# First mean layer of a four-layer graph network: products made in the normalising stage, gathered by the edge sums

## The reference, cut to what matters

```python
x1 = layernorm(x + L0(x, ...))            # (50000, 128)

def sage_conv(h, src, dst, n, W_self, W_neigh, b):
    agg  = segment_sum(h[src], dst, n)
    deg  = segment_sum(ones, dst, n)
    mean = agg / maximum(deg, 1.0)[:, None]
    return h @ W_self + mean @ W_neigh + b

h1 = relu(sage_conv(x1, src, dst, n, W_self1, W_neigh1, b1))   # the part that changes
x2 = layernorm(x1 + sage_conv(h1, src, dst, n, W_self2, W_neigh2, b2))
```

## Time and profile before

| | us |
|---|---|
| median of 3 runs (8755.55 to 8763.08) | 8756.22 |
| the profiled execution | 8752.19 |
| its span | 8750.5 |

### The profile page before, as it was taken

The page is one execution under the profiler, slowest core; times in us unless marked ns, Lnnn a source line. Parts: engine busy times, 40 slices in busy tenths (PEclk is TensorE's granted clock), DMA queues, the critical chain, the costliest instruction groups (busy, mean ns, idle before and its releaser), DMA issues. The chain is left out here.

```text
span 8750.5 us, 136064 instructions
## 1 busy us (share of the span) xinstructions
PE 5075.0 (58%) x26949; PEld 3942.2 (45%) x26950; DVE 4064.5 (46%) x13584; ACT 2826.8 (32%) x6967; POOL 4235.5 (48%) x4934
## 2 busy tenths in 40 slices
PE   3666667705679556965785567544444444414577
PEld 2555444504568445854564455333322233303555
DVE  3555558861222122755662227544444444452458
ACT  0544452361343124841331248311111111100239
POOL 4777750056630565036615664555555555507650
PEclk7766679955789567976896679666666666655679
DMA  1222225572358223943574458311111111122348
GB/s 31 65 66 66 67 60 173 183 242 64 93 156 248 70 85 116 337 161 101 156 230 120 118 169 288 117 49 53 47 48 49 48 48 48 48 20 61 90 149 295
DMA packets 610422, 1013.48 MB, mean 116 GB/s; under 512 B 174962, under 2 KB 177296, under 8 KB 610064
## 3 DMA queue, kind: packets, MB, share of 16 engines
q1 hardware_dynamic: 279472, 417.77, 16.1%
q10 hardware_dynamic: 197568, 359.75, 11.6%
q0 software_dynamic: 133280, 234.88, 10.9%
HBM read 648.88 MB, written 363.07 MB: 116 GB/s over the span
## 5 line engine op out<-in xcount | busy, mean ns | idle before, releaser
L447 PE MATMUL agg_bank<-agg_msgs,agg_onehot 128*128 x7840 | 1573.5, 361 | 976.0 <-issue 697.9
L447 PEld LDWEIGHTS agg_bank<-agg_msgs,agg_onehot 128*128 128x128 f32 x7840 | 1344.7, 256 | 1273.3 <-issue 1263.5
L385 DVE TENSOR_TENSOR agg_onehot<-iota,rel 128x512 f32<-128x512 f32 x1176 | 814.3, 692 | 1717.5 <-issue 630.3
L316 POOL DMA_INDIRECT agg_msgs<-y,agg_rows x784 | 784.3, 1000 | 409.3 <-issue 210.9
L1446 PE MATMUL score_look<-score_rounded,score_loT 128*128 128x392 bf16 x392 | 178.5, 455 | 716.9 <-ACT score_loT L1515 535.1
L1398 POOL DMA_INDIRECT by_source<-score_line,score_places x392 | 397.3, 1013 | 261.7 <-DVE score_line L1572 152.7
L482 ACT ACTIVATE agg_kept<-agg_bank,inv_root 128x128 f32<-128x128 f32 x784 | 226.5, 367 | 879.9 <-PE agg_bank L447 453.5
L1093 POOL DMA_INDIRECT mlp_xs<-in_x,mlp_rows x392 | 396.6, 1012 | 233.5 <-issue 152.0
L482 ACT ACTIVATE agg_kept<-agg_bank,inv_deg 128x128 f32<-128x128 f32 x784 | 224.2, 368 | 875.2 <-PE agg_bank L447 665.4
L447 PE MATMUL agg_bank<-agg_weighted,agg_onehot 128*128 x1568 | 349.5, 394 | 265.4 <-DVE agg_onehot L385 137.5
L313 POOL DMA_INDIRECT agg_weight<-weights,agg_rows x392 | 408.9, 1043 | 182.2 <-issue 111.5
(11 more groups left out here) (333 smaller groups left out, 12898.8 us busy)
## 6 DMA issues: line engine op xcount, KB each, us to landing
sums<-agg_kept ACTq DMA_DIRECT2D x588, 256.0 KB
agg_first<-y ACTq DMA_DIRECT2D x196, 256.0 KB
messages<-mlp_m SPq DMA_DIRECT2D x98, 256.0 KB
agg_first<-in_x ACTq DMA_DIRECT2D x98, 256.0 KB
agg_msgs<-messages SPq DMA_DIRECT2D x98, 256.0 KB
l_z<-sums SPq DMA_DIRECT2D x98, 256.0 KB
x<-l_o POOLq DMA_DIRECT2D x98, 256.0 KB
l1a_s<-sums SPq DMA_DIRECT2D x98, 256.0 KB
```

The source lines that it names most:

```text
L316: pool.indirect_dma_start(msgs[:, j, :], None, table[:, :], bass.IndirectOffsetOnAxis(ap=rows[:, third, j:j + 1], axis=0)).then_inc(sm[f"g ...
L385: nc.vector.tensor_tensor(onehot[:, j, :, :], k.iota[:, 0:P].unsqueeze(1).to_broadcast([P, Q, P]), k.rel[:, ds(i * (4 * Q) + j * Q, Q)].un ...
L447: t.matmul(bank[:, column[q], :], onehot[:, j, q, :], messages[:, slot[q], :], start=False, stop=True, skip_group_check=True)\
```

## The change

The weights are applied before the edges are summed, not after, and the division by the degree is done last:

relu(x1 Ws + b + (sum x1[src]) / d Wn) = relu((d (x1 Ws + b) + sum (x1 Wn)[src]) / d), with d = max(deg, 1).

The stage l0 becomes `normalise_project`: after it has normalised a group it transposes it, multiplies it by both weights, and stores three tables: `x1`, `near` = x1 Wn, and `start` = d (x1 Ws + b). "agg1" gathers rows of `near`, fills its banks with `start`, scales by `inv_deg`, ends in relu and writes `h1`. The stage `sage_hidden` is gone. `count_in` keeps d in `k.degree`.

```diff
-def aggregate(nc, k, name, table, rows_of_edges, out, before=None, scale=None, tally=None, weights=None):
+def aggregate(nc, k, name, table, rows_of_edges, out, before=None, scale=None, tally=None, weights=None, floor=False):
...
-                    c.link(v.tensor_scalar(k.inv_deg[:, :], counts[:, 0:NT], 1.0, None, ALU.max))
+                    c.link(v.tensor_scalar(k.degree[:, :], counts[:, 0:NT], 1.0, None, ALU.max))
...
-                    c.link(v.reciprocal(k.inv_deg[:, :], k.inv_deg[:, :]))
+                    c.link(v.reciprocal(k.inv_deg[:, :], k.degree[:, :]))
...
-                            last = a.activation(kept[:, u, q, :], bank[:, u * Q + q, :], ACT.Copy, scale=scale[:, ds(g * Q + q, 1)])
+                            last = a.activation(kept[:, u, q, :], bank[:, u * Q + q, :], ACT.Relu if floor else ACT.Copy, scale=scale[:, ds(g * Q + q, 1)])
...
-def sage_hidden(nc, k, ins, sums, x1, h1):
...
-def normalise_nodes(nc, k, name, z_rows, out):
...
+def normalise_project(nc, k, ins, z_rows, x1, near, start):
...
             @block.sync
+                def load(i, u):
+                    g = i * D + u
+                    if after(i, u, D, D):
+                        sp.wait_ge(sm["normed"], g - (D - 1))
+                        sp.wait_ge(sm["normed_more"], g - (D - 1))
                     sp.dma_start(z[:, u, :, :], rows_of(z_rows, g)).then_inc(sm[f"z{u}"], 16)
+                def store_products(i, u):
+                    g = i * D + u
+                    sp.wait_ge(sm["kept"], g + 1)
+                    sp.dma_start(rows_of(near, g), near_o[:, u, :, :]).then_inc(sm[f"near_out{u}"], 16)
+                    sp.wait_ge(sm["scaled"], g + 1)
+                    sp.dma_start(rows_of(start, g), start_o[:, u, :, :]).then_inc(sm[f"start_out{u}"], 16)
+                def body(i, u):
+                    for lag, step in ((0, load), (8, store_products)):
...
             @block.gpsimd
+                    for q in range(2, Q):
+                        last = nc.gpsimd.tensor_scalar(o[:, u, q, :], z[:, u, q, :], rstd[:, u, q:q + 1], shift[:, u, q:q + 1], ALU.mult, ALU.add)
+                    last.then_inc(sm["normed_more"], 1)
...
             @block.vector
+                def scale_start(i, u):
+                    g = i * D + u
+                    dve.wait_ge(sm["product"], g + 1)
+                    if after(i, u, D, D):
+                        dve.wait_ge(sm[f"start_out{u}"], i * 16)
+                    v.tensor_tensor(start_o[:, u, :, :], pS[u % 2][:, :, :], k.degree[:, ds(g * Q, Q)].unsqueeze(2).to_broadcast([P, Q, C]), ALU.mult)\
+                     .then_inc(sm["scaled"], 1)
+                def body(i, u):
+                    for lag, step in ((0, moments), (1, scales), (5, scale_start)):
...
+            @block.tensor
+                def turn(i, u):
+                    g = i * D + u
+                    pe.wait_ge(sm["normed"], g + 1)
+                    pe.wait_ge(sm["normed_more"], g + 1)
+                    if after(i, u, 2, D):
+                        pe.wait_ge(sm["copied"], g - 1)
+                    for q in range(Q):
+                        last = t.transpose(pT[u % 2][:, q, :], o[:, u, q, :], k.ident[:, :])
+                    last.then_inc(sm["turned"], 1)
+                def products(i, u):
+                    g = i * D + u
+                    pe.wait_ge(sm["copied"], g + 1)
+                    if after(i, u, 2, D):
+                        pe.wait_ge(sm["kept"], g - 1)
+                        pe.wait_ge(sm["scaled"], g - 1)
+                    t.matmul(pS[u % 2][:, :, :], k.ones_b[0:3, :], k.bias[0:3, BIASES.index("L1_gnn_b1"), :, :], start=True, stop=True)
+                    for q in range(Q):
+                        t.matmul(pN[u % 2][:, q, :], oT[:, u % 2, q, :], wn[:, :], start=True, stop=True)
+                        last = t.matmul(pS[u % 2][:, q, :], oT[:, u % 2, q, :], ws[:, :], start=False, stop=True, skip_group_check=True)
+                    last.then_inc(sm["product"], 1)
+                def body(i, u):
+                    for lag, step in ((0, turn), (1, products)):
...
             @block.scalar
+                    for q in range(2):
                         last = a.activation(o[:, u, q, :], z[:, u, q, :], ACT.Identity, scale=rstd[:, u, q:q + 1], bias=shift[:, u, q:q + 1])
+                def copy(i, u):
+                    g = i * D + u
+                    act.wait_ge(sm["turned"], g + 1)
+                    if after(i, u, 2, D):
+                        act.wait_ge(sm["product"], g - 1)
+                    a.activation(oT[:, u % 2, :, :], pT[u % 2][:, :, :], ACT.Copy).then_inc(sm["copied"], 1)
+                def keep(i, u):
+                    g = i * D + u
+                    act.wait_ge(sm["product"], g + 1)
+                    if after(i, u, D, D):
+                        act.wait_ge(sm[f"near_out{u}"], i * 16)
+                    a.activation(near_o[:, u, :, :], pN[u % 2][:, :, :], ACT.Copy).then_inc(sm["kept"], 1)
+                def body(i, u):
+                    for lag, step in ((0, root), (1, normalise), (3, copy), (5, keep)):
...
-        normalise_nodes(nc, k, "l0", sums, x1)
-        aggregate(nc, k, "agg1", x1, k.src_row, sums, scale=k.inv_deg)
-        sage_hidden(nc, k, ins, sums, x1, h1)
+        normalise_project(nc, k, ins, sums, x1, near, start)
+        aggregate(nc, k, "agg1", near, k.src_row, h1, before=start, scale=k.inv_deg, floor=True)
```

More of the change, by code:

```diff
@@ L765, in _ @@
             def _(sp):
-                def body(i, u):
[L767 to L773, removed]
+                sp.dma_start(wn[:, :], ins["L1_gnn_W_neigh1"]).then_inc(sm["w"], 16)
@@ L775, in _ @@
+                def body(i, u):
+                    for lag, step in ((0, load), (8, store_products)):
+                        if live(*before_by(i, u, lag, D), D):
+                            step(*before_by(i, u, lag, D))
+                all_of(sp, body, 8)
+                for u in range(D):
+                    sp.wait_ge(sm[f"near_out{u}"], 16 * len(range(u, GROUPS, D)))
+                    sp.wait_ge(sm[f"start_out{u}"], 16 * len(range(u, GROUPS, D)))
             @block.gpsimd
             def _(pool):
-                def body(i, u):
-                    if live(i, u, NODES_DEEP):
-                        g = i * NODES_DEEP + u
-                        pool.wait_ge(sm["shift"], g + 1)
-                        if after(i, u, NODES_DEEP, NODES_DEEP):
-                            pool.wait_ge(sm[f"written{u}"], i * 16)
-                        pool.sem_inc(sm["pass_pool"], 1)
-                        nc.gpsimd.tensor_scalar(o[:, u, Q - 1, :], z[:, u, Q - 1, :], rstd[:, u, Q - 1:Q], shift[:, u, Q - 1:Q], ALU.mult, ALU.add)\
-                          .then_inc(sm["normed_last"], 1)
-                    i, u = before_by(i, u, 1, NODES_DEEP)
-                    if live(i, u, NODES_DEEP):
-                        g = i * NODES_DEEP + u
-                        pool.wait_ge(sm["normed"], g + 1)
-                        pool.wait_ge(sm["normed_last"], g + 1)
-                        pool.dma_start(rows_of(out, g), o[:, u, :, :]).then_inc(sm[f"written{u}"], 16)
@@ L793, in _, with normalise @@
-                rounds(pool, body, 1, deep=NODES_DEEP)
-                for u in range(NODES_DEEP):
-                    pool.wait_ge(sm[f"written{u}"], 16 * len(range(u, GROUPS, NODES_DEEP)))
+                def normalise(i, u):
+                    g = i * D + u
+                    pool.wait_ge(sm["shift"], g + 1)
+                    if after(i, u, D, D):
+                        pool.wait_ge(sm[f"written{u}"], i * 16)
+                        pool.wait_ge(sm["turned"], g - (D - 1))
+                    pool.sem_inc(sm["pass_pool"], 1)
+                    for q in range(2, Q):
+                        last = nc.gpsimd.tensor_scalar(o[:, u, q, :], z[:, u, q, :], rstd[:, u, q:q + 1], shift[:, u, q:q + 1], ALU.mult, ALU.add)
+                    last.then_inc(sm["normed_more"], 1)
@@ new lines, in store @@
+                def store(i, u):
+                    g = i * D + u
+                    pool.wait_ge(sm["normed"], g + 1)
+                    pool.wait_ge(sm["normed_more"], g + 1)
+                    pool.dma_start(rows_of(x1, g), o[:, u, :, :]).then_inc(sm[f"written{u}"], 16)
+                def body(i, u):
+                    for lag, step in ((0, normalise), (1, store)):
+                        if live(*before_by(i, u, lag, D), D):
+                            step(*before_by(i, u, lag, D))
@@ L797, in _ @@
+                all_of(pool, body, 1)
+                for u in range(D):
+                    pool.wait_ge(sm[f"written{u}"], 16 * len(range(u, GROUPS, D)))
             @block.vector
@@ L827, in _, with moments @@
-                rounds(dve, body, 1, deep=NODES_DEEP)
+                def moments(i, u):
+                    g = i * D + u
+                    dve.wait_ge(sm[f"z{u}"], i * 16 + 16)
+                    for q in range(Q):
```

(57 more changed lines are left out.)

61 lines of the change are left out of this document (32 added, 29 removed).

## The result

| | before | after |
|---|---|---|
| median of the runs, us | 8755.88 (8748.25 to 8763.08, 4 runs) | 8536.73 (8521.04 to 8551.33, 4 runs) |
| the profiled execution, us | 8752.19 | 8521.04 |
| ratio | | 0.9743, 95% interval 0.9728 to 0.9757 |

The kernel is 219 us faster. On a second chip, with seven runs of the kernel before beside four of the changed one, the ratio was 0.9718 (0.9702 to 0.9735).

A forecast was written before the change was run, and what follows sets the result against it. Stages between barriers bound the kernel, and the DMA was to set the new l0. Removing l1a -321.1, new l0 +153.9 and agg1 +5.4 gave -161.8 us: forecast 8593 us, range 8542 to 8650.

The forecast's parts named there:

- What goes, 321.1 us: Stage l1a, barrier to barrier with its loads and store, disappears whole: 321.1 us less.
- the sums, +5.4: agg1 starts its banks from a table and scales at the end, as agg4 does: +5.4 us.
- PE's 2.73 us: New l0, TensorE: l1a's work less four transposes, 2.73 us a group, second behind the DMA.
- DVE's 2.34: New l0, DVE: the present 1.65 us period plus one multiply out of PSUM at 0.692, 2.34 us a group.
- ACT's 2.45: New l0, ACT: one root, two normalising ACTIVATEs, two copies out of PSUM at 0.597, 2.45 us a group.
- The DMA's 3.22: New l0: one load and three stores, 1 MB a group, take 3.22 us and set the stage's period.
- The split between loads and stores: DMA prices solved from the l0 and l1b windows: 340 GB/s for loads, 327 for stores at full share.
- Edges 19.5: New l0's time beyond its 98 group periods, taken as in the old l0: 19.5 us, ends 16 and 30.
- Rival 1: DMA is not the ceiling; PE's 2.73 sets new l0's period, stage 287.0, kernel 8542 to 8546 us; chance 0.14.
- Rival 2: Stores in new l0's mix are dearer: period 3.4 to 3.8, stage 353 to 392, kernel 8608 to 8648; chance 0.20.
- rival 3: Slower than before: SP's store step stands in front of its loads in new l0, e.g. 8784 us; chance 0.05.
- The rule weighed: l1b's 330 GB/s read as ceiling, against the skill's 425 (2.47 us a group) or 341 (3.07); trace agrees with the lower.

The follow-up runs named there:

- fill_relu: Kernel before with only agg1 changed, its banks starting from x1 and ending in relu: agg1 629.6 us, agg2 of the same run 623.2.
- mixes: DMA alone, network left out: seven stages of 98 groups, four 256 KB transfers a group in different load/store mixes; 264.1 to 274.2 us a stage.
- l1b_store: Kernel before with one more 256 KB store a group in l1b, from an unchanging tile: stage l1b 341.4 us against 330.6.
- no_bias: Changed kernel without the bias matmul in the new l0, b1 left out of the result, all DMAs kept: stage l0 283.5 us.

## Why the prediction was wrong

The step that failed is the price of the DMA, in the prediction's words: "The l1b window moves 330 GB/s at a share of 0.98, which I read as the ceiling", and "Share over rate is DMA time per byte". It made 3.22 us a group where 2.736 were measured. The trace of the kernel before could have shown it: in none of the windows of l0, l1b and l3 in the earlier trace rows does an engine wait for a landing, and over the whole of l1b PE waited for one for 0.7 us (its weight loads for 1.1):

```profile
L914 PE MATMUL l1b_pS<-ident,l1b_s 128*128 128x128 f32 x391 | 92.3, 276 | 0.7 <-DMA l1b_own<-h 0.7
```

Point by point:

- **What goes, 321.1 us; the sums, +5.4.** Right: l1a is gone whole, agg1 took +5.5, and fill_relu, which fills from a table and ends in relu, took as much.
- **PE's 2.73 us.** Right to the hundredth (2.736); it was named as second, and it holds the period, with the DMA within 1% of it.
- **DVE's 2.34, ACT's 2.45.** The multiply took 692 ns as its row had it. With both limits lowered the period is (247.5 - 17.1) / 98 = 2.35 us. PE is busy 99.26 of 100 there and DVE 87.44; whether PE or DVE's 2.34 holds it is open. ACT's 2.45 was too high: in that run it is busy 87.53 of 100, 2.06 us a group. The copies out of PSUM take 578 ns, not 597, and records of ACTIVATEs that follow each other overlap: two normalising ones of 0.48 us span 0.88 together.
- **The DMA's 3.22.** Wrong: its own period is 2.70 to 2.74, and the stage's 2.736. Rates of windows in which engines set the pace were divided by their shares. The mixes show a full DMA as 1.02 to 1.05 at 381 to 406 GB/s; the new l0 and its variants read 0.84 at 288, 0.97 at 333 and 1.03 at 384. Between the first and the last the share grows by a factor of 1.23 and the rate by 1.33, so the share is no measure of the room left. 98 x (3.22 - 2.73) is 48 of the 50 us.
- **The split between loads and stores** (340 and 327) had the wrong level, and its form failed too: the mixes do not follow one price for each kind.
- **Edges 19.5.** 17.1 measured, the other 2 us.
- **Rival 1** (PE's 2.73 sets the period, 0.14) gave the right time for l0, 287.0 against 285.2, and most of the right reason; its sign, a period of 2.73 without gaps on PE, is what came. It said that a true DMA limit was nowhere shown, which was the right objection. What it did not see is that the DMA's limit, at 2.70 to 2.74 us, lies within 1% or so of PE's: that the two meet is chance. The range ended at 8542, the very time of this rival, so it had no room for it to be a few us off. Rival 2 is out with a period under 3.4; rival 3 too: SP waited for ACT's copy in front of its loads, 48.0 us in 200, but no engine waited for a load.
- **The rule weighed.** The Trainium skill (DMA: Bandwidth & Descriptors, section Bandwidth) gives 425 GB/s for 16 MB and 341 for 1 MB. The prediction had the trace agree with the lower; the mixes, with 256 KB transfers queued back to back, lie between, at 381 to 406.

## What to carry to other kernels

A DMA share near 1 says that transfers are nearly always under way, not that no more would fit: before a rate is taken as a ceiling, ask whether in that window the engines waited for landings; where no engine waits for a load, the window shows no DMA limit. PE's busy share has the same fault: it read 100.00 of 100 at two different periods of l1b_store, so the period of a group is what to compare. When a new stage is priced by several resources, write down the period of each with the ends of its own uncertainty: two of them can meet, and then relieving one gives next to nothing until the other is relieved too.

## What the runs showed of the hardware

Stages made of direct transfers and matmuls took nearly the same time on every chip (l0 285.2, 286.0, 285.6 us; l1b 329 to 331; l1a 321.1, 321.7 and 324.8 in the three profiles that have it), while the stages of indirect gathers did not. On the chip where the kernel before took 7614.6 us, agg1 of no_bias took 530.6 us against 622.2, with gathers as long on POOL (979 against 992 ns) but far less waiting for the buffers to come free. First that run, then the changed kernel on the first chip:

```profile
POOL agg_msgs L317 <- PE agg_bank L448: 17.8, 57, 0.9
```

```profile
POOL agg_msgs L317 <- PE agg_bank L448: 76.8, 38, 4.4
```

The waits there are up to 4.4 us long on the first chip and 0.9 on the other. Why buffers come free later on one chip than on another no run here settles. The whole kernel before took 7614.6 us against 8755.9, five times what the change gives; that the difference lies in the stages with gathers is seen in the changed kernels, since that run of the kernel before has no profile.
